# Spectra from sums and differences of mirrored steps, with new orders in the preparation and the routing

## Chip, cores and metric

The kernel runs on one core of a Trainium2 chip. The metric is the device time of one execution in microseconds (us). Before the change the median of 3 runs is 1136.09 us.

## The reference, cut to what matters

`x` is 2 x 512 x 512 and the context 2 x 8192 x 512, all in float32. Three layers are added to `x` one after the other. `LN` is a layer normalization over the last axis.

```
q, k, v = linear(linear(LN(x))), linear(linear(ctx)), ...
x = x + linear(softmax(q k^T / sqrt(512)) v + q)          # attention over 8192 steps
xn = LN(LN(x)) * ln_g + ln_b                              # state-space layer, 512 steps
u, z = split(xn @ in_w.T + in_b);  z = silu(z)
kernel[l, d] = sum_n exp(l * logA[d, n]) * C[d, n] * B[d, n] * dt[d]
y = irfft(rfft(u, 1024) * rfft(kernel, 1024))[:512]       # causal convolution over the steps
x = x + clip((y * z) @ out_w.T + out_b + LN(x), -10, 10)
e = argmax(softmax(LN(x) @ gate_w + gate_b))              # one of 8 experts for each token
x = x + LN(x) @ expert_w[e] + expert_b[e]
```

## The kernel before

Every large matrix product is made in three passes: an operand is split into a rounded part (`hi`) and a remainder (`lo`), both of type fp32r, and `PASSES` multiplies hi by hi, hi by lo and lo by hi. ScalarE writes the hi part from a PSUM bank, VectorE (DVE in the profile) subtracts it to make the lo part, and TensorE (PE) goes on with both. A product tile of 128 x 512 with a contraction of 512 is 12 matmuls. GpSimd (POOL) makes some lo parts from data in SBUF, and issues the gathers and scatters of the routing.

Each engine has an order written out by hand, with semaphores between them. `JOBS` lists the uses of the 8 PSUM banks in order, and `open_bank` makes TensorE wait until the use of the same bank 8 jobs earlier has been emptied (`evacuated` counts VectorE's, `copied` ScalarE's). The stages are:

- **Preparation** (`prepare`, 0 to about 148 us). Weights are folded into each other. TensorE transposes `qW`, makes `x_to_q`, transposes the normalized rows of batch 0 (`xT0`), makes the queries `q0`, transposes the rows of batch 1 (`xT1`), and makes `q_to_ctx`, `q1` and so on. `first_norm` on VectorE is 16 small instructions on 4 to 8 elements and four large ones. GpSimd meanwhile makes lo parts of `cW` (`lo_tiles`) and then the table of cosines and sines (`transform_table`, 31 us of small steps, result `dft`).
- **Attention of batch 0**, 64 steps of 24 matmuls each. Beside it ScalarE and VectorE sum the filter `kern` in 64 terms (`add_term`, counted by `term_added`).
- **Middle** (about 509 to 573 us). `turn_pooled` transposes the attention result and the input weights, `kernT` transposes the filter, `attend` adds the attention to `x`, `kernel_spectra` makes 8 spectra of the filter, the new rows are normalized and transposed (`normT`), then come `u`, `z` and `input_spectra(0)`, another 8 spectra.
- **Attention of batch 1**, with the complex products of batch 0 (`output_products`) on GpSimd.
- **Tail** (from about 929 us). The same for batch 1, with the products on VectorE (`outputs`, 20 instructions for each half of the frequencies), inverse transforms (`in_time`), the output projection (`project_out`), the last normalization, the choice of an expert for each token (`gate_logits`, `gate`, `route`), and 15 groups of 128 tokens: each is gathered, transposed (`turn_tokens`), multiplied with its expert's weights (`mix`) and scattered to the output.

The 512 steps are taken in two halves of 256 (`U0` and `U1`, for the filter `Ka` and `Kc`, from which `Ks` is made), each with a cosine and a sine part at 256 frequencies from the table `dft`. `spectrum` contracts over 256 steps, two tiles of 128:

```
for t in range(2):
    for a, c in PASSES:
        last = nc.tensor.matmul(dst[:], dft[:, a, t, m * P:(m + 1) * P], src[:, c, first + t, :], ...)
```

Of the kernel before, what the change touches and what calls it, by code (L numbers as in the profile page):

```python
# [12 lines left out]
P = 128  # L13
# [7 lines left out]
E = 8  # L21
# [47 lines left out]
def spectrum_jobs(b):  # L69
# [4 lines left out]
PREP_JOBS = (tiles("qWT", "x_to_q", "xT0") + ["vectors"] + tiles("kWT", "q0", "xT1", "q_to_ctx", "q1", "qc0", "vWT", "qc1")  # L74
# [10 lines left out]
             + ["logits@0"] + tiles_at(1, "ffnT")[2:] + ["logits@1", "logit_columns", "ranks", "slots"] + MIX_JOBS)  # L85
# [32 lines left out]
LOADS = [("hW", 1), ("oW", 0)]  # L118
# [10 lines left out]
def build(nc, x, ctx_in, hW, hb, cW, cb, qW, qb, kW, kb, vW, vb, oW, ob, A_log, B_param, C_param, log_dt,  # L129
          in_w, in_b, out_w, out_b, ln_g, ln_b, gate_w, gate_b, expert_w, expert_b, out):  # L130
    with ExitStack() as ctx:
# [39 lines left out]
        ident = sb("ident", [P, P])  # L171
        obB = sb("obB", [P, D])
# [60 lines left out]
        hit_group = h[1][:, 0:B * T * 2 * E].rearrange("p (i g) -> p i g", g=2 * E)  # L233
# [5 lines left out]
        sign = sb("sign", [P, 2])  # L239
        logA = sb("logA", [P, NS, T])  # L240
# [10 lines left out]
        in_q = [sem(f"in_q{half}") for half in range(2)]  # L251
        in_stage = [sem(f"in_stage{n}") for n in range(8)]
# [24 lines left out]
        u_biased = sem("u_biased")  # L277
        u_hi, u_lo = [sem(f"u_hi{b}") for b in range(B)], [sem(f"u_lo{b}") for b in range(B)]
# [70 lines left out]
        def evacuated_by(eng, name):  # L349

            if name in COPIED:
                eng.wait_ge(copied, COPIED[name])
            else:
                eng.wait_ge(evacuated, EVAC[name])

# [79 lines left out]
        def _(sp):  # L435
            def load(name, src):
                sp.dma_start(raw[BUF[name]][:], src).then_inc(in_stage[BUF[name]], 16)
# [4 lines left out]
            load("hW", matrix(hW))  # L442
# [163 lines left out]
            fixed_load(2)  # L606
            fixed_load(4)
            store_x(0)
            fixed_load(3)
# [17 lines left out]
        def _(pe):  # L627
# [47 lines left out]
            def turn_rows(job, src, k):  # L675
                dst = open_bank(job)
                for t in range(T):
                    last = nc.tensor.transpose(dst[:, t * P:(t + 1) * P], src[:, k, t * P:(t + 1) * P], ident[:])  # L678
# [7 lines left out]
            def prepare():  # L686
# [18 lines left out]
                products("q0.#", hlC, hlD)  # L705
                row_transposes("xT1.#", resid0, ROWS["x1"])
                split_of("cW")
                products("q_to_ctx.#", hlF, hlE)
# [123 lines left out]
            def spectrum(job, m, src, first):  # L832

                dst = open_bank(job)
                for t in range(2):
                    for a, c in PASSES:
                        last = nc.tensor.matmul(dst[:], dft[:, a, t, m * P:(m + 1) * P], src[:, c, first + t, :],  # L837
# [1443 lines left out]
```

## Time and profile before

| | before |
|---|---|
| median of 3 runs, us | 1136.09 (1134.95 to 1138.33) |
| the profiled execution, us | 1134.54, with a span of 1132.8 from its first to its last instruction |
| TensorE busy | 1093.9 us, 97% of the span |
| VectorE busy | 841.3 us, 74% |
| ScalarE, GpSimd busy | 530.5 and 537.5 us, 47% each |
| mean granted TensorE clock | 0.985 of full speed |

The profile lists, for each instruction or run of equal ones, its start, its length, its engine and line, the tile that it writes and those that it reads, and in brackets how long its engine stood idle before it and what ended that. A row with `x4` covers four instructions.

### The profile page before, as it was taken

To read this page: it belongs to the slowest core of one execution; us is meant where nothing else is said; L and a number is where in the kernel's file an instruction comes from. 1 tells how busy PE (TensorE), PEld (TensorE's weight loads), DVE (VectorE), ACT (ScalarE), POOL (GpSimd) and SP (SyncE) were. 2 spreads that over 40 slices of the span, in tenths; PEclk is the share of its full clock that TensorE was granted. 3 is DMA by queue.
4 is the path that set the end of the run, shared out by engine and by line. 5 is a ranking of instruction groups with operands and counts; after the bars stand their busy time and mean duration, and the time that the engine had idled before them with its cause. 6 is when DMAs were issued, how large, how long until landed. Compare 5 with 4: busy or idle time off the path is not lost.

```text
span 1132.8 us, 16497 instructions
## 1 busy us (share of the span) xinstructions
PE 1093.9 (97%) x4969; PEld 884.5 (78%) x4969; DVE 841.3 (74%) x1756; ACT 530.5 (47%) x1127; POOL 537.5 (47%) x588
## 2 busy tenths in 40 slices
PE   7999999999999999999999999999999999998498
PEld 5787877878888888888888888888888888886375
DVE  6963498799888888778357777776777657699584
ACT  4221056556555555533464444444444444356462
POOL 3700445345444544411266666665765632177253
PEclk8999999999999999999999999999999999999699
DMA  8211368977876787432429767766876541025991
GB/s 292 84 53 59 52 153 211 218 194 190 204 179 185 190 192 195 140 87 99 76 73 203 193 187 202 187 191 171 213 185 177 179 161 38 1 76 161 323 398 66
DMA packets 199351, 182.26 MB, mean 161 GB/s; under 512 B 17873, under 2 KB 144881, under 8 KB 199299
## 3 DMA queue, kind: packets, MB, share of 16 engines
q1 hardware_dynamic: 178658, 140.21, 48.3%
q10 hardware_dynamic: 17280, 31.46, 7.9%
q0 software_dynamic: 3360, 9.97, 2.4%
q8 instruction: 24, 0.39, 0.1%
q14 instruction: 29, 0.23, 0.1%
HBM read 141.73 MB, written 41.68 MB: 162 GB/s over the span
## 4 chain that ended last, share of the span: by engine, by line
PE 80%; DVE 8%; POOL 4%; DMA 3%; issue 3%; SPq 1%; ACT 1%; POOLq 0%; ACTq 0%; DVEq 0%
PE bank L644 39%; PE bank L783 28%; PE bank L1040 4%; PE bank L837 3%; PE bank L652 1%; PE bank L1026 1%; DMA stage<-in_L_xattn_hW_dram 1%; DVE h L1527 1%; DMA stage<-in_L_ffn_expert_w_dram 1%; DMA spectra<-in_ctx_dram 1%; PE bank L987 1%; PE bank L678 1%; POOL hl_C L2023 1%; PE bank L1045 1%; POOL hl_B L2039 1%
## 5 line engine op out<-in xcount | busy, mean ns | idle before, releaser
L1187 ACT ACTIVATE probs<-bank,nbias 128x512 f32<-128x512 f32 x128 | 88.1, 688 | 242.3 <-DVE nbias L1650 242.1
L783 PE MATMUL bank<-hl_F,probsT 128*128 128x512 f32 x768 | 190.4, 397 | 0.6 <-issue 0.4
L783 PE MATMUL bank<-hl_A,probsT 128*128 128x512 f32 x768 | 190.4, 396 | 0.0
L644 PE MATMUL bank<-hl_B,hl_D 128*128 128x512 f32 x768 | 185.7, 391 | 1.8 <-POOL hl_B L2039 1.4
L1645 DVE TENSOR_REDUCE mx<-bank 128x1 f32<-128x512 f32 x128 | 88.0, 687 | 133.9 <-PE bank L644 133.9
L644 PE MATMUL bank<-hl_C,hl_D 128*128 128x512 f32 x768 | 185.3, 390 | 0.0
L783 PEld LDWEIGHTS bank<-hl_F,probsT 128*128 128x128 f32 x768 | 144.1, 188 | 35.4 <-issue 0.8
L783 PEld LDWEIGHTS bank<-hl_A,probsT 128*128 128x128 f32 x768 | 144.1, 188 | 34.3 <-POOL hl_A L2032 0.2
L644 PEld LDWEIGHTS bank<-hl_B,hl_D 128*128 128x128 f32 x768 | 143.7, 188 | 34.1 <-issue 2.3
L644 PEld LDWEIGHTS bank<-hl_C,hl_D 128*128 128x128 f32 x768 | 144.1, 188 | 31.7 <-issue 0.3
L2032 POOL TENSOR_TENSOR hl_F<-stage,hl_F 128x512 fp32r<-128x512 f32 x64 | 84.7, 1323 | 162.2 <-ACT hl_F L1152 162.1
L2032 POOL TENSOR_TENSOR hl_A<-stage,hl_A 128x512 fp32r<-128x512 f32 x64 | 84.2, 1315 | 145.4 <-ACT hl_A L1152 145.4
L1691 DVE SCALAR_TENSOR_TENSOR rows<-rows,alpha,bank 128x512 f32<-128x512 f32 x128 | 90.9, 710 | 14.9 <-PE bank L783 14.9
L1662 DVE TENSOR_TENSOR probsT<-bank,probsT 128x512 fp32r<-128x512 f32 x128 | 87.3, 682 | 1.9 <-ACT probsT L1174 1.8
L1174 ACT ACTIVATE probsT<-bank 128x512 fp32r<-128x512 f32 x128 | 74.2, 580 | 10.8 <-PE bank L770 10.7
L1152 ACT ACTIVATE hl_F<-stage 128x512 fp32r<-128x512 f32 x64 | 40.4, 632 | 27.7 <-issue 18.2
L1152 ACT ACTIVATE hl_A<-stage 128x512 fp32r<-128x512 f32 x64 | 40.4, 632 | 27.6 <-issue 18.3
L2039 POOL TENSOR_TENSOR hl_C<-spectra,hl_C 128x512 fp32r<-128x512 f32 x32 | 40.9, 1292 | 22.9 <-ACT hl_C L1160 22.9
L2039 POOL TENSOR_TENSOR hl_C<-xb,hl_C 128x512 fp32r<-128x512 f32 x32 | 41.0, 1292 | 20.2 <-ACT hl_C L1160 20.2
L1667 DVE STREAM_TRANSPOSE bank<-resid 128x512 f32<-128x512 f32 x60 | 43.0, 716 | 9.4 <-DMA resid<-p_rows 9.4
L1683 DVE SCALAR_TENSOR_TENSOR lsum<-lsum,alpha,rsum 128x1 f32<-128x1 f32 x128 | 49.0, 383 | 0.0
L1699 DVE SCALAR_TENSOR_TENSOR zT<-h,cbdt,zT 128x512 f32<-128x512 f32 x64 | 46.6, 728 | 0.0
(419 smaller groups left out, 1862.6 us busy)
## 6 DMA issues: line engine op xcount, KB each, us to landing
p_rows<-probs ACTq DMA_DIRECT2D x120, 256.0 KB, 3.1
stage<-in_ctx_dram SPq DMA_DIRECT2D x112, 256.0 KB, 3.2
spectra<-in_ctx_dram SPq DMA_DIRECT2D x64, 256.0 KB, 5.9
xb<-in_ctx_dram SPq DMA_DIRECT2D x64, 256.0 KB, 5.9
resid<-p_rows SPq DMA_DIRECT2D x240, 64.0 KB, 2.1
h<-p_rows SPq DMA_DIRECT2D x120, 64.0 KB, 2.5
obB<-p_rows SPq DMA_DIRECT2D x120, 64.0 KB, 2.0
stage<-in_L_ffn_expert_w_dram SPq DMA_DIRECT2D x6, 1024.0 KB, 6.9
```

Of the source, the lines that this page charges most:

```text
L644: last = nc.tensor.matmul(dst, lhs[:, a, t, k * P:(k + 1) * P], rhs[:, c, t, :], start=(t == 0 and (a, c) == PASSES[0]), stop=(t == T - 1 ...
L783: last = nc.tensor.matmul(obank[u % 2][:], probsT[u % 2][:, a, j, :], nat[b][par][:, c, j, :], start=(j == 0 and (a, c) == PASSES[0]), sto ...
L1152: nc.scalar.activation(nat[b][par][:, 0, j, :], stage[par][:, j, :], ACT.Copy).then_inc(nat_hi, 1)
L1174: nc.scalar.activation(dst, src, ACT.Copy).then_inc(pT_hi, 1)
L1187: nc.scalar.activation(dst, src, ACT.Exp, bias=nbias[:, q:q + 1], scale=SCALE, accum_out=rsum[:, q:q + 1]).then_inc(probs_ready, 1)
L1645: nc.vector.tensor_reduce(mx[:, col], sbank[u % 2][:], AX_X, ALU.max).then_inc(stat_done, 1)
L1662: nc.vector.tensor_tensor(lo, src, hi, ALU.subtract).then_inc(pT_split, 1)
L1683: nc.vector.scalar_tensor_tensor(lsum[:, col], lsum[:, col], alpha[:, u:u + 1], rsum[:, col], ALU.mult, ALU.add).then_inc(sums_updated, 1)
L1691: nc.vector.scalar_tensor_tensor(rows[:, q, :], rows[:, q, :], alpha[:, u:u + 1], obank[u % 2][:], ALU.mult, ALU.add).then_inc(rows_added, 1)
L1699: nc.vector.scalar_tensor_tensor(kern[:, k, :], h[u % 2][:], weight, kern[:, k, :], ALU.mult, ALU.add).then_inc(term_added, 1)
L2032: nc.gpsimd.tensor_tensor(nat[b][par][:, 1, j, :], stage[par][:, j, :], nat[b][par][:, 0, j, :].bitcast(F32), ALU.subtract).then_inc(nat_s ...
L2039: nc.gpsimd.tensor_tensor(by_squares(ctxT[par][:, 1])[:, dd], square(squares[b][par], dd), by_squares(ctxT[par][:, 0])[:, dd].bitcast(F32) ...
```

## The change

1. **Spectra.** The two tiles of 128 steps of each half are first added and subtracted, with the nearer one in mirrored order. The sums give the cosine part and the differences the sine part, so `spectrum` contracts over 128 rows, 3 matmuls instead of 6, for all 24 spectra. The mirrored order comes for free in the transposes of the normalized rows (`flip` in place of `ident` for even tiles), in the lags of the filter (`lag_ramp`), in the reading of `z` (`gates`, two instructions instead of one) and in the inverse table (`inverse_table`, six instructions instead of four).
2. **Sums and differences** on VectorE: `fold_kernel` (4 instructions ahead of `lift(0)`), `inputs` (4 more) and `inputs_in_place` (4 more).
3. **The filter spectra** are turned in phase, by 8 instructions on ScalarE (`spectrum_parts`) and 8 on VectorE (`turn_spectra`), which wait for each other.
4. **The table** is half as large, and is made after both normalizations of the preparation (GpSimd waits for `rows_ready`); `lo_tiles("cW")` waits for the first one.
5. **Preparation:** `hW` is loaded in 4 transfers; `q_to_ctx` comes ahead of `xT1` on all engines.
6. **Tail:** the lo parts of `gated_hl[0]` move from GpSimd to VectorE; GpSimd's masks need two short instructions, and its lo parts of `W0` wait for the last product; SyncE loads `W3` ahead of `W4`; ScalarE rounds `W3` between two sums of rows; `gate_logits(1)` is one part, and the logits of batch 0 are turned ahead of it.
7. **Routing:** the first 8 groups are placed by `place_at(rank)` before the overflow groups are worked out; their gathers start at `indexed` 1. `split_expert_bias` moves behind `route`. `turn_tokens(1)` comes inside `mix(0)`.

```diff
-PREP_JOBS = (... + tiles("kWT", "q0", "xT1", "q_to_ctx", "q1", "qc0", "vWT", "qc1")
+PREP_JOBS = (... + tiles("kWT", "q0", "q_to_ctx", "xT1", "q1", "qc0", "vWT", "qc1")
...
             # sync
-            load("hW", matrix(hW))
+            load_tiles(stage[1], matrix(hW), in_h)        # for t in range(T): sp.dma_start(dst[:, t], src[:, t])
...
             fixed_load(1)
             fixed_load(2)
+            fixed_load(3)
             fixed_load(4)
             store_x(0)
-            fixed_load(3)
...
             # tensor
-            def spectrum(job, m, src, first):
+            def spectrum(job, m, src, n):
                 dst = open_bank(job)
-                for t in range(2):
-                    for a, c in PASSES:
-                        last = nc.tensor.matmul(dst[:], dft[:, a, t, m * P:(m + 1) * P], src[:, c, first + t, :], ...)
+                for a, c in PASSES:
+                    last = nc.tensor.matmul(dst[:], dft[:, a, 0, m * P:(m + 1) * P], src[:, c, n, :], ...)
...
             def middle():
                 turn_pooled(0)
-                pe.wait_ge(term_added, TERMS)
-                transposes("kernT.#", kern)
+                turn_kernel()                             # waits for kern_folded 4
...
-                gate_logits(1, 2)
-                turn_logits()
+                turn_logits(0)
+                gate_logits(1, 1)
+                turn_logits(1)
                 rank_tokens()
-                place_tokens()
+                place_tokens("slots.0", 1, 0, E)
+                place_tokens("slots.1", 2, E, E)
                 turn_tokens(0)
                 for g in range(GROUPS):
-                    if g + 1 < GROUPS:
+                    if 0 < g < GROUPS - 1:
                         turn_tokens(g + 1)
                     mix(g)                                # mix(0) calls turn_tokens(1) after its first tile
...
             # scalar
+            def spectrum_parts():
+                for c in range(2):
+                    for n, m in enumerate((Ka, Ks)):
+                        ...
+                        if c + n > 0:
+                            act.wait_ge(spectrum_turned, 2 * (2 * c + n))
+                        nc.scalar.activation(probs[0][:], m[:, 2 + c, :], ACT.Copy, scale=turn[:, 2 + c:3 + c]).then_inc(part_put, 1)
+                        nc.scalar.activation(probs[1][:], m[:, c, :], ACT.Copy, scale=turn[:, 2 + c:3 + c]).then_inc(part_put, 1)
...
                 weights(1)
                 weights(2)
-                for t in range(2, T):
-                    sum_rows(t)
+                sum_rows(2)
+                weights(3)
+                sum_rows(3)
                 means()
-                weights(3)
...
             # vector
             def inputs():
-                for k in range(T):
-                    filled_by(dve, f"u.{k}@0")
-                    nc.vector.tensor_tensor(uT[:, k, :], bank_of(f"u.{k}@0")[:], ubB[:], ALU.add).then_inc(evacuated, 1)
+                for n in range(2):
+                    near, far = 2 * n, 2 * n + 1
+                    for k in (near, far):
+                        filled_by(dve, f"u.{k}@0")
+                        nc.vector.tensor_tensor(uT[:, k, :], bank_of(f"u.{k}@0")[:], ubB[:], ALU.add).then_inc(evacuated, 1)
+                    dve.wait_ge(evacuated, EVAC[f"u.{far}@0"])
+                    nc.vector.tensor_tensor(h[n][:], uT[:, far, :], uT[:, near, :], ALU.add).then_inc(u_folded, 1)
+                    nc.vector.tensor_tensor(uT[:, far, :], uT[:, far, :], uT[:, near, :], ALU.subtract).then_inc(u_folded, 1)
+
+            def fold_kernel():
+                dve.wait_ge(term_added, TERMS)
+                for n in range(2):
+                    ...
+                    nc.vector.tensor_tensor(h[n].rearrange("p (t m) -> p t m", t=T), far, near, ALU.add).then_inc(kern_folded, 1)
+                    nc.vector.tensor_tensor(far, far, near, ALU.subtract).then_inc(kern_folded, 1)
+
+            def turn_spectra():
+                for n in range(2 * 2):
+                    c, m = n // 2, (Ka, Ks)[n % 2]
+                    cosine = turn[:, c:c + 1]
+                    dve.wait_ge(part_put, 2 * n + 2)
+                    nc.vector.scalar_tensor_tensor(m[:, c, :], m[:, c, :], cosine, probs[0][:], ...).then_inc(spectrum_turned, 1)
+                    nc.vector.scalar_tensor_tensor(m[:, 2 + c, :], m[:, 2 + c, :], cosine, probs[1][:], ...).then_inc(spectrum_turned, 1)
...
             def middle():
+                fold_kernel()
                 lift(0)
...
                 lo_rows("normT.#@0", hlF)
+                turn_spectra()
                 inputs()
...
             # vector, tail
                 gate_output(0, range(2, T))
-                outputs(1, range(1, 5))
+                outputs(1, range(1, 3))
+                for k in range(T):
+                    gated_lo(0, k)
+                outputs(1, range(3, 5))
...
                 scale_outputs()
-                split_expert_bias()
                 gate()
                 route()
+                split_expert_bias()
...
             # vector, route
-                nc.vector.tensor_reduce(rank, hit_value, AX_X, ALU.add)
+                link(nc.vector.tensor_reduce(rank, hit_value, AX_X, ALU.add))
+                place_at(rank)
...
+                filled_by(dve, "slots.0")
+                nc.vector.tensor_scalar(gather_rows[:, 0:E], bank_of("slots.0")[:, 0:E], ...).then_inc(indexed, 1)
...
             # gpsimd
+            pool.wait_ge(rows_ready, ROWS["x0"] + 1)
             lo_tiles("cW", zT, hlE)
+            pool.wait_ge(rows_ready, ROWS["x1"] + 1)
             transform_table()
...
                 add_out_bias(0)
-                gated_lo()
                 routing_masks()
+                pool.wait_ge(product_step, PRODUCTS * (TRIPS + 2))
+                lo_tiles("W0", raw[BUF["W0"]], weights_hl[0])
                 add_out_bias(1)
```

## Rows read from the trace of the kernel before

**Rows 1.** The page: TensorE's busy time, share of the span and instructions.

```profile
PE 1093.9 (97%) x4969; PEld 884.5 (78%) x4969; DVE 841.3 (74%) x1756; ACT 530.5 (47%) x1127; POOL 537.5 (47%) x588
```

**Rows 2.** Timeline, TensorE in the preparation (start, length, what, idle before).

```profile
29.90 11.20 PE L644 MATMUL bank<-hl_D,hl_C 128*128 128x512 f32 x48 [0.31 <-DVE hl_D L1464]
...
43.53 2.91 PE L678 MATMUL bank<-ident,resid 128*128 128x128 f32 x16 [2.44 <-DVE hl_F L1421]
...
46.09 12.27 PE L644 MATMUL bank<-hl_E,hl_F 128*128 128x512 f32 x48
...
58.19 11.04 PE L644 MATMUL bank<-hl_D,hl_C 128*128 128x512 f32 x48
```

**Rows 3.** Timeline of all engines, 10 to 17 us.

```profile
10.46 2.19 ACT L1112 ACTIVATE hl_B<-stage 128x512 fp32r<-128x512 f32 x4 [1.64 <-DMA stage<-in_L_xattn_hW_dram]
...
11.86 13.90 PE L644 MATMUL bank<-hl_A,hl_B 128*128 128x512 f32 x48 [4.08 <-DVE hl_B L1509]
...
16.65 1.22 DVE L1489 TENSOR_SCALAR seed<-var 128x4 int32<-128x4 int32 x1
```

**Rows 4.** Timeline of VectorE, about 40 us.

```profile
39.55 3.23 DVE L1498 TENSOR_SCALAR resid<-xb,mv,rstd 128x512 f32<-128x512 f32 x4
...
42.70 2.47 DVE L1421 TENSOR_TENSOR hl_F<-bank,hl_F 128x512 fp32r<-128x512 f32 x4
```

**Rows 5.** Windows in the preparation (busy by engine, PEclk, DMA share, GB/s).

```profile
10.00:15.00 5.00, 3.14 (x7) 2.48 (x8) 3.88 (x7) 2.19 (x4) 0.00 (x0) 0.59 1.04 390
...
45.00:50.00 5.00, 5.00 (x20) 4.12 (x19) 4.96 (x8) 2.48 (x5) 4.76 (x6) 0.66 0.48 173
```

**Rows 6.** Timeline of the middle stage, 509 to 563 us.

```profile
509.76 0.75 DVE L1691 SCALAR_TENSOR_TENSOR rows<-rows,alpha,bank 128x512 f32<-128x512 f32 x1 [3.81 <-PE bank L783]
...
516.55 11.13 PE L644 MATMUL bank<-hl_E,hl_A 128*128 128x512 f32 x48
...
527.52 11.05 PE L837 MATMUL bank<-hl_F,dft 128*128 128x512 f32 x48
...
532.35 1.91 DVE L1498 TENSOR_SCALAR rows<-xb,mv,rstd 128x512 f32<-128x512 f32 x4
...
538.60 0.75 DVE L1790 SCALAR_TENSOR_TENSOR qc<-resid,sign,bank 128x512 f32<-128x512 f32 x1 [0.55 <-PE bank L837]
...
540.41 11.18 PE L644 MATMUL bank<-hl_B,hl_F 128*128 128x512 f32 x48
...
552.36 0.63 ACT L1262 ACTIVATE hl_A<-spectra 128x512 fp32r<-128x512 f32 x1 [2.09 <-DVE spectra L1764]
...
553.07 1.29 POOL L2145 TENSOR_TENSOR hl_A<-spectra,hl_A 128x512 fp32r<-128x512 f32 x1 [1.43 <-ACT hl_A L1262]
...
562.31 11.04 PE L837 MATMUL bank<-hl_A,dft 128*128 128x512 f32 x48
```

**Rows 7.** Timeline of the tail, up to the first wait for outputs.

```profile
978.17 1.29 DVE L376 TENSOR_TENSOR probs<-qc,spectra 128x512 f32<-128x512 f32 x2 [2.59 <-issue]
...
1001.54 1.67 DVE L376 TENSOR_TENSOR spectra<-probs,obB 128x512 f32<-128x512 f32 x1
...
1012.07 0.98 PE L875 MATMUL bank<-probsT,hl_B 128*128 128x256 f32 x6 [0.22 <-DVE hl_B L1810]
```

**Rows 8.** Timeline of the tail, from the expert weights to the first mix.

```profile
1035.95 2.19 ACT L1341 ACTIVATE hl_F<-stage 128x512 fp32r<-128x512 f32 x4 [3.54 <-DMA stage<-in_L_ffn_expert_w_dram]
...
1040.23 3.59 PE L987 MATMUL bank<-spectra,gate_raw 128*8 128x512 f32 x8 [2.82 <-ACT spectra L1224]
...
1053.71 0.22 DVE L1906 TENSOR_TENSOR ssm_in<-onehot,bank 128x64 f32<-128x64 f32 x1 [1.58 <-PE bank L1010]
...
1057.19 1.22 DVE L1928 TENSOR_TENSOR dft<-ssm_in,ssm_w 128x1024 fp32r<-128x1024 f32 x1
...
1060.37 0.17 DVE L1932 TENSOR_SCALAR gather_rows<-bank 128x15 int32<-128x15 f32 x1 [1.06 <-PE bank L1017]
...
1069.69 4.28 PE L1040 MATMUL bank<-hl_C,probsT 128*128 128x512 f32 x12
```

More of the change, by code:

```diff
@@ L71, in spectrum_jobs @@
     return at(b, *[f"{n}.{c}" for c in range(2) for n in ("U0r", "U0i", "U1r", "U1i")])
-PREP_JOBS = (tiles("qWT", "x_to_q", "xT0") + ["vectors"] + tiles("kWT", "q0", "xT1", "q_to_ctx", "q1", "qc0", "vWT", "qc1")
+PREP_JOBS = (tiles("qWT", "x_to_q", "xT0") + ["vectors"] + tiles("kWT", "q0", "q_to_ctx", "xT1", "q1", "qc0", "vWT", "qc1")
              + tiles("ctx_to_v", "oWT") + ["key_row.0", "key_row.1", "x_bias", "key_bias"] + tiles("ctx_to_x", "qo0")
@@ L84 @@
              + tiles_at(0, "x_ssm")[2:] + tiles_at(1, "x_ssm") + tiles_at(0, "ffnT") + tiles_at(1, "ffnT")[:2]
-             + ["logits@0"] + tiles_at(1, "ffnT")[2:] + ["logits@1", "logit_columns", "ranks", "slots"] + MIX_JOBS)
+             + ["logits@0"] + tiles_at(1, "ffnT")[2:] + ["logits@1", "logit_columns", "ranks", "slots.0", "slots.1"] + MIX_JOBS)
 JOBS = PREP_JOBS + MID_JOBS + TAIL_JOBS
@@ L251, in build @@
         in_q = [sem(f"in_q{half}") for half in range(2)]
+        in_h = [sem(f"in_h{t}") for t in range(T)]
         in_stage = [sem(f"in_stage{n}") for n in range(8)]
@@ L435, in _, with load_tiles @@
         def _(sp):
+            def load_tiles(dst, src, landed):
+                for t in range(T):
+                    sp.dma_start(dst[:, t], src[:, t]).then_inc(landed[t], 16)
             def load(name, src):
@@ L705, in prepare @@
                 products("q0.#", hlC, hlD)
+                split_of("cW")
+                evacuated_from("kWT.3")
+                products("q_to_ctx.#", hlF, hlE)
                 row_transposes("xT1.#", resid0, ROWS["x1"])
-                split_of("cW")
-                products("q_to_ctx.#", hlF, hlE)
                 evacuated_from("xT1.3")
@@ L1010, in rank_tokens, with place_tokens @@
                 nc.tensor.matmul(dst[:, B * T * E:2 * B * T * E], ones, flat, start=True, stop=True).then_inc(filled, 1)
-            def place_tokens():
-                pe.wait_ge(ranked, 1)
-                dst = open_bank("slots")
+            def place_tokens(job, count, first, width):
+                pe.wait_ge(ranked, count)
+                dst = open_bank(job)
                 for n in range(B * T):
-                    last = nc.tensor.matmul(dst[:, 0:2 * E], place[:, n, :], numbered[:, n, :], start=(n == 0), stop=(n == B * T - 1))
+                    last = nc.tensor.matmul(dst[:, 0:width], place[:, n, :], numbered[:, n, first:first + width],
+                                            start=(n == 0), stop=(n == B * T - 1))
                 last.then_inc(filled, 1)
@@ L1041, in mix @@
                                          start=(t == 0 and (a, c) == PASSES[0]), stop=False)
+                    if g == 0 and t == 0:
+                        turn_tokens(1)
                 if g == 0:
```

231 lines of the change are left out of this document (138 added, 93 removed).

## The prediction

> **What bounds the kernel now.** I read the page first. TensorE is busy for 97% of the span [rows 1]. The two attention passes are long runs of matmuls that the change does not touch, so the whole gain or loss lies in the preparation, the middle and the tail. For these I read the timeline engine by engine, looking for the wait that TensorE ends on, because a matmul that is removed is worth something only where TensorE does not then wait for VectorE.
>
> Preparation: the first products start 4.08 us late, on the lo part of `hW` [rows 3]. The clock was granted at 0.59 in that stretch [rows 5], so 48 matmuls take 13.90 us where the same 48 take 11.20 later [rows 2]. A second idle time of 2.44 us stands ahead of `xT1`; then the clock is 0.66 [rows 5] and 48 matmuls take 12.27 us [rows 2]. Middle: TensorE is nearly gapless, but the `u` products at 540.41 end a VectorE path (attention added, statistics, rows, four filter spectra, lo part), since `normT` ends on VectorE [rows 6]. Tail: VectorE runs the products one after the other from 978.17 [rows 7], and TensorE meets it at 1012.07. Then logits wait 2.82 us for ScalarE, which had stood idle 3.54 us for `W3` [rows 8].
>
> **The change part by part.** One matmul is 11.04 / 48 = 0.230 us [rows 6]. 24 spectra lose 3 each: 72 x 0.230 = 16.6 us of TensorE. How much is kept must be worked out by stage.
>
> *Preparation.* (a) `hW` by tiles. ScalarE waited 1.64 us for the one transfer and started at 10.46; VectorE's first lo part came 0.66 later and the product at 11.86 [rows 3]. With tiles landing in turn, the start is set by VectorE, which is done with `qWT` about 1.3 us before that product. So 1.3 us, and a busy TensorE should be back at full clock sooner: of the 13.90 - 11.20 = 2.7 us that the slow clock costs, I take 1.3 back. From both sides: 0 (all tiles land as late as the one) and 1.3 + 2.7 = 4.0. I take 2.6 at the start of `q0`.
> (b) GpSimd waits for both normalizations. In the first, a `TENSOR_SCALAR` on 4 elements took 1.22 us and the next three about as much, while GpSimd worked; a `TENSOR_SCALAR` of that size takes 0.17 when it doesn't (the one at 1060.37) [rows 8]. That hides under TensorE. In the second, the four large ones took 3.23 us [rows 4] against 1.91 for the same four at 532.35 [rows 6]. VectorE starts it about 2.6 us earlier by (a), and gains 1.3 + 1.0 on the way, so the lo parts of `kWT`, at 42.70 [rows 4], start near 37.8 and end 2.47 later, at 40.3.
> (c) `q_to_ctx` goes first. It needs those lo parts, so it starts at 40.3 in place of 46.09 [rows 2]. `q0` ends near 29.90 - 2.6 + 11.1 = 38.4, so 1.9 us of idling remain, less than the 2.44 that was followed by a slow clock; I take full clock. It ends at 51.4; `xT1` takes 1.9 us; then `q1` needs its last lo part (0.6 on ScalarE, 0.7 on VectorE): start at 54.6 against 58.19. **Gain 3.6 us**. If the clock falls, 12.27 - 11.04 = 1.2 to 1.7 us less. Everything behind, the loads of squares too, hangs on this chain and shifts with it. The table ends near 37.7 + 26 = 64, and is first needed at about 82; with no cover it would cost nothing until it took 44 us.
>
> *Middle.* (d) `fold_kernel`, four instructions with an effective 0.62 (2.47 / 4) [rows 4] = 2.5 us, stands ahead of `lift(0)` on VectorE, after the row at 509.76. The transposes of the weights use banks that VectorE empties, so `attend` at 516.55 slides to about 519. (e) Filter spectra: 24 x 0.230 = 5.5 us less on TensorE. But `u` hangs on VectorE: from 527.52, where `attend` ends, to the first `u` product at 540.41 are 12.9 us. Without waiting for spectra, VectorE needs 532.35 + 1.91 - 527.52 = 6.7 for statistics and rows, 4 x 0.69 for the filter spectra (0.75 each alone, row at 538.60) and 0.7 for the lo part: 10.2. 12.9 - 10.2 = 2.7, minus the 2.5 of (d): **gain 0.2**. Bounds: -2.5 (the fold fully exposed) and 3.0. (f) Input spectra: 5.5 us less, if the sums and differences are there. After the lo parts of `normT` (about 542), phase turning is four rounds of two ScalarE (0.63 + 0.55) and two VectorE instructions (0.74 + 0.66), 2.7 us each, the first round's ScalarE part covered: VectorE is free at 551.5. `inputs` is 8 x 0.62 + 0.1 = 5.1: 556.6. Then ScalarE 0.63 (at 552.36) and GpSimd 1.29 (at 553.07) [rows 6] for the last tile, with the tile before it queued: 559.8. The spectra start at 562.3 and want the second half 1.4 later; cover is 3.9 us, and the `z` products are what hides it. ScalarE then has `gates` (1.3 + 4 x 0.95) behind the rounding: until 564.6, and 8 copies of 0.52: 568.8, while TensorE needs the fourth at 567.8 to go on. **Gain 5.4 us**. Bounds 0 to 5.5.
>
> The Trainium skill (SBUF — State Buffer, Who interferes with whom) says that a VectorE instruction with two SBUF inputs and a GpSimd instruction that reads SBUF exclude each other for the whole instruction. By that, the sums and differences could each wait for one of GpSimd's lo parts; the sum with two such waits would put the last tile at 562.4, still within the cover.
>
> *Tail.* (g) The third set of spectra saves 5.5 us that VectorE does not use: it starts its products only when the first two spectra are copied. `inputs_in_place` ends 1.3 later than now, its ScalarE partner starts earlier; the products start at 977.8, 0.4 us early. 28 instructions later nothing has changed; then four lo parts are added (4 x 0.6 = 2.4), and the waits go that GpSimd caused: 1.67 us for a 0.69 us instruction at 1001.54 [rows 7], 3.1 us in all. The second outputs are ready near 1010.6, where TensorE meets them at 1012.07 [rows 7]: **1.4 us**. Bounds -2 and 5. (h) `W3` is issued some 15 us earlier, so the 2.82 us of waiting at 1040.23 go [rows 8], minus 0.9 because `gate_logits(1)` now waits for all its tiles: **1.9 us**, bounds 0 and 2.8. With (g) and 0.1 the ranks come 3.4 us early. (i) Routing. Before, from the first instruction on the ranks at 1053.71 to `gather_rows` at 1060.37 are 6.7 us [rows 8]. After: 0.6, then `place_at` 1.22 (the 1057.19 row), TensorE's 8 matmuls 1.9 with three short links beside them, so 3.8 us: 2.9 early. But VectorE must then work out the overflow (3.5), wait for `slots.1` (2) and split the bias (2.6), free at ranks + 12.4, when the first gathered tile wants its lo part at ranks + 11.4. `mix(0)` starts at ranks + 13.1 against 1069.69 - 1053.71 = 16.0 now: 2.9, less 0.9 for `turn_tokens(1)` inside it: **2.0 us**, bounds 0 and 3. Its 14 followers run at TensorE's pace and keep it.
>
> Sum: 3.6 + 0.2 + 5.4 + 1.4 + 1.9 + 0.1 + 2.0 = 14.6 us. The profiled execution took 1134.54, 1.55 below the median of 1136.09: 1134.54 - 14.6 = 1119.9, and for the median 1121.5. I predict **1121.5 us**.
>
> **Rivals.**
> - *Phase turning is not hidden.* If a round takes 3.9 us in place of 2.7, the cover of 3.9 is gone, and from there each microsecond of a round costs four. With rounds of 5.3 the whole 5.4 is lost: 1127. Against: all durations have rows. Chance 12%.
> - *`hW` gains nothing.* Three more issues on SyncE (0.46 us each) push `x[0]` and `cW` back, and the DMA share is 1.04 in that stretch [rows 5], so tiles may land no sooner. Then (a) is 0 and `q0` starts at 29.9; (b) and (c) keep a part: 1124.0. Chance 15%. The Trainium skill (SBUF — State Buffer, Summary: rules for kernel authors) asks for one transfer on 128 partitions and not several; by that rule this case would be the likeliest.
> - *Routing gives back.* VectorE's later bias split, or the stores of the rows that the gathers wait for, end last: (i) and (h) are 0, 1125.5. Chance 8%.
> - *Slower.* In the attention passes VectorE has about 0.5 us free in a step of 5.54. If the second pass is entered in another phase to GpSimd, and one short instruction per step is caught behind a GpSimd one (1.22 in place of 0.17 is 1.05) [rows 3, 8], the step grows by 0.55: 64 x 0.55 = 35 us, 1156. It decides from 15 us / 64 = 0.23 us a step. Nothing in the first pass, entered from another side, shows it. Chance 3%.
> - *The change doesn't do what it says*: TensorE falls back to a pace of one copy per spectrum. A copy is 0.60 against 3 x 0.230 = 0.69; it would need to be longer. Chance 2%, counted with the first.
>
> **How the numbers follow.** Forecast 58% (1118.5 to 1124.0), the rivals 14, 15, 8 and 3%, and 2% for better than all. The range reaches to the phase-turning rival and to the upper bounds of (a), (e), (g): **1115.5 to 1127.5**. What a measurement of this kernel can tell from no change is about 0.3%, 3.4 us. Only parts of the middle rivals together end within it: faster 94%, same 3%, slower 3%.
>
> **What would show it.** `q1` starts near 54.6. `attend` starts 2 to 3 us later relative to the end of attention, `u` at the same distance, the second attention pass 5.5 us sooner. Input spectra have no idle time ahead of them. In the tail, the product rows are all 0.69. `gather` starts 6 us after the onehot, not 9. I am wrong if TensorE waits for `u_lo` ahead of the input spectra, if the PEclk falls in a stretch where it was 1.00, or if steps of attention are longer than 5.54.

## The result, and the profile after

The changed kernel took 1126.13 us (median of 5; 1124.40 to 1128.57), the kernel before 1136.08 in the same comparison: ratio 0.9917, 95% interval 0.9901 to 0.9933. In a second comparison (after_again, below) it was 0.9914 (0.9894 to 0.9933). The medians are 9.9 us apart in both comparisons, and the ratios make it 9.4 and 9.8 us, where 14.6 were forecast: in the range of 1115.5 to 1127.5, but 2.1 us above the 1118.5 to 1124.0 to which the forecast gave 58%. The profiled execution is the one of 1126.13; its span is 1124.3 against 1132.8 (an execution 1.5 us below its median), so 8.5 us are to be found in the trace.

The page, TensorE's line, against [rows 1]:

```profile
PE 1081.0 (96%) x4897; PEld 873.5 (78%) x4897; DVE 846.6 (75%) x1784; ACT 535.8 (48%) x1145; POOL 523.0 (47%) x583
```

TensorE lost 12.9 us of busy time and the kernel 8.5. Timeline of TensorE in the preparation:

```profile
10.33 12.52 PE L657 MATMUL bank<-hl_A,hl_B 128*128 128x512 f32 x48 [2.52 <-DVE hl_B L1562]
...
26.65 11.17 PE L657 MATMUL bank<-hl_D,hl_C 128*128 128x512 f32 x48
39.96 12.75 PE L657 MATMUL bank<-hl_E,hl_F 128*128 128x512 f32 x48 [2.15 <-DVE hl_F L1474]
52.55 1.91 PE L692 MATMUL bank<-ident,resid 128*128 128x128 f32 x16
56.52 12.80 PE L657 MATMUL bank<-hl_D,hl_C 128*128 128x512 f32 x48 [2.06 <-DVE hl_D L1517]
69.16 3.11 PE L657 MATMUL bank<-hl_A,hl_B 128*128 128x512 f32 x13
```

`q0` starts 3.25 us sooner than in [rows 2], `q_to_ctx` (39.96) 6.1 sooner, `q1` (56.52) only 1.7 sooner, and `qc0` starts at 69.16 against 69.07 before. Two idle times of 2.1 us now stand where one of 2.44 stood, and both products behind them are slow. Windows of TensorE (busy, count, granted clock, DMA share, GB/s):

```profile
42.00:44.00 2.00, 2.00 (x6) 0.51 0.74 264
44.00:46.00 2.00, 2.00 (x11) 1.00 0.92 318
58.00:60.00 2.00, 2.00 (x6) 0.50 0.00 0
```

Six matmuls in 2 us at 0.5 (1.2 GHz), eleven at 1.00 (2.4 GHz). Timeline of VectorE ahead of `q1`:

```profile
53.39 0.69 DVE L1486 TENSOR_TENSOR hl_B<-bank,hl_B 128x512 fp32r<-128x512 f32 x1 [2.04 <-ACT hl_B L1095]
53.99 2.48 DVE L1517 TENSOR_TENSOR hl_D<-bank,hl_D 128x512 fp32r<-128x512 f32 x4
```

The four lo parts of `xT1` can't begin before the last one of `q_to_ctx`, and TensorE waits for all four. Timeline of the middle:

```profile
509.83 0.75 DVE L1744 SCALAR_TENSOR_TENSOR rows<-rows,alpha,bank 128x512 f32<-128x512 f32 x1 [3.81 <-PE bank L799]
...
514.00 3.19 PE L665 MATMUL bank<-ident,stage 128*128 128x128 f32 x16 [2.47 <-DVE hl_B L1525]
...
519.36 11.14 PE L657 MATMUL bank<-hl_E,hl_A 128*128 128x512 f32 x48
530.34 5.60 PE L852 MATMUL bank<-hl_F,dft 128*128 128x512 f32 x24
...
540.37 11.17 PE L657 MATMUL bank<-hl_B,hl_F 128*128 128x512 f32 x48 [1.20 <-DVE hl_F L1517]
...
544.89 0.75 DVE L1839 SCALAR_TENSOR_TENSOR qc<-qc,turn,probs 128x512 f32<-128x512 f32 x1 [1.47 <-ACT probs L1273]
...
556.50 1.77 DVE L1822 TENSOR_TENSOR spectra<-spectra 128x512 f32<-128x512 f32 x1
...
559.38 1.30 POOL L2251 TENSOR_TENSOR hl_A<-spectra,hl_A 128x512 fp32r<-128x512 f32 x1
562.26 5.60 PE L852 MATMUL bank<-hl_A,dft 128*128 128x512 f32 x24
567.70 2.66 PE L657 MATMUL bank<-hl_B,hl_D 128*128 128x512 f32 x11
```

Against [rows 6]: `attend` 2.8 later, `u` where it was, input spectra without an idle time ahead of them and half as long. The second attention starts 5.49 us sooner (567.70; 573.19 before) and takes 358.66 us to the transposes of its last rows, where it took 358.74. Timeline of the tail:

```profile
971.99 1.29 DVE L385 TENSOR_TENSOR probs<-qc,spectra 128x512 f32<-128x512 f32 x2 [1.41 <-ACT spectra L1250]
...
1004.95 0.98 PE L899 MATMUL bank<-probsT,hl_B 128*128 128x256 f32 x6 [1.48 <-DVE hl_B L1895]
...
1030.74 3.59 PE L1010 MATMUL bank<-spectra,gate_raw 128*8 128x512 f32 x8
...
1039.88 0.59 ACT L1277 ACTIVATE h<-bank 8x512 f32<-8x512 f32 x1 [3.77 <-PE bank L1010]
...
1044.52 0.22 DVE L1992 TENSOR_TENSOR ssm_in<-onehot,bank 128x64 f32<-128x64 f32 x1 [0.80 <-PE bank L1033]
...
1048.42 0.17 DVE L2002 TENSOR_SCALAR gather_rows<-bank 128x8 int32<-128x8 f32 x1 [1.45 <-PE bank L1040]
...
1050.83 1.24 POOL L2297 DMA_INDIRECT spectra<-mixed,gather_rows  x1 [19.21 <-DMA mixed<-zT]
...
1057.28 1.09 PE L1050 MATMUL bank<-ident,spectra 128*128 128x128 f32 x4 [3.14 <-DMA spectra<-mixed,gather_rows]
...
1059.87 1.62 PE L1064 MATMUL bank<-hl_C,probsT 128*128 128x512 f32 x3 [1.50 <-DVE probsT L2052]
...
1065.42 0.49 PE L1071 MATMUL bank<-dft,selected 16*128 16x512 f32 x1
```

Against [rows 7, 8]: the second outputs come 7.1 us sooner, the ranks 9.2, the gather's indices 11.9, but `mix(0)` 9.8, and its last matmul (1065.42) 8.5, since it was at 1073.89. The gather was released by a store (`mixed<-zT`), not by its indices.

| us ahead of before, at | measured | forecast |
|---|---|---|
| `qc0` (end of the preparation's chain) | -0.1 | 3.6 |
| `u` | 0.0 | 3.8 |
| second attention | 5.5 | 9.2 |
| second outputs | 7.1 | 10.6 |
| ranks | 9.2 | 12.6 |
| end of `mix(0)` | 8.5 | 14.6 |

### The profile page after: what moved, and what is told of

Same layout as the page of the kernel before. It is cut to its first block, busy times and chain, and to the rows that moved or that the text cites. A ratio compares the mean times of both kernels' runs of the same rounds, so it can differ in the third digit from the quotient of the medians.

```text
span 1124.3 us, 16407 instructions
## 1 busy us (share of the span) xinstructions
PE 1081.0 (96%) x4897; PEld 873.5 (78%) x4897; DVE 846.6 (75%) x1784; ACT 535.8 (48%) x1145; POOL 523.0 (47%) x583
## 4 chain that ended last, share of the span: by engine, by line
PE 79%; DVE 11%; issue 4%; POOL 2%; DMA 2%; ACT 1%; SPq 1%; POOLq 0%; ACTq 0%; DVEq 0%
PE bank L657 41%; PE bank L799 28%; PE bank L1064 4%; PE bank L665 1%; DVE probs L385 1%; PE bank L1050 1%; DVE h L1580 1%; PE bank L1010 1%; DMA spectra<-in_ctx_dram 1%; PE bank L1071 1%; POOL hl_B L2137 1%; DMA resid<-p_rows 1%; PE bank L743 0%; POOL hl_F L2130 0%; PE bank L852 0%
## 5 line engine op out<-in xcount | busy, mean ns | idle before, releaser
L1168 ACT ACTIVATE h<-resid,logA 128x512 f32<-128x512 f32 x64 | 45.4, 709 | 0.0
```

## The experiments

### Preparation

**ctx_last**: the order alone undone, on TensorE, ScalarE and VectorE.

```diff
-tiles("kWT", "q0", "q_to_ctx", "xT1", "q1", ...
+tiles("kWT", "q0", "xT1", "q_to_ctx", "q1", ...
...
                 products("q0.#", hlC, hlD)
+                row_transposes("xT1.#", resid0, ROWS["x1"])
                 split_of("cW")
-                evacuated_from("kWT.3")
                 products("q_to_ctx.#", hlF, hlE)
-                row_transposes("xT1.#", resid0, ROWS["x1"])
...                                                   # ScalarE and VectorE in the same order
```

> Undoes one edit of the preparation, the order: xT1 is turned ahead of q_to_ctx again, hW by tiles and GpSimd's two waits stay. Theory (the new order costs the gain): q0 ends at 37.8 us as now; the transposes of xT1 need only the banks that VectorE frees with the lo parts of kWT from 38.1 on, so TensorE idles about 0.3 us and not 2.15, xT1 ends near 40.4, q_to_ctx takes 11.04 at full clock and q1 starts near 51.5 in place of 56.52: 5.0 us faster than the changed kernel, 1121. Rival 1 (the order is worth something, and the gain was lost to other work): q1 starts at 56.5 or later, time unchanged or up to 2 us longer. Rival 2 (the clock falls near 40 us whatever the order, with the burst of loads that begins there): q_to_ctx takes 12.3 to 12.8 although TensorE hardly idled, q1 at 53, 3.4 us faster.

1119.98 us, ratio 0.9882 (0.9866 to 0.9899). Timeline of TensorE:

```profile
38.30 2.42 PE L692 MATMUL bank<-ident,resid 128*128 128x128 f32 x16 [0.35 <-DVE hl_F L1473]
40.76 11.12 PE L657 MATMUL bank<-hl_E,hl_F 128*128 128x512 f32 x48
51.72 11.04 PE L657 MATMUL bank<-hl_D,hl_C 128*128 128x512 f32 x48
62.60 11.04 PE L657 MATMUL bank<-hl_A,hl_B 128*128 128x512 f32 x48
```

`q1` at 51.72 as expected, `qc0` at 62.60: 6.56 us sooner than in the changed kernel, 4.80 by `q1`'s start and 1.76 by its clock. Another 1.6 of it is the clock of `q_to_ctx` (12.75 for 11.12), so the order by itself costs 3.2 us. By the ratios (0.9917 and 0.9882, two chips) it is 4.0 us, with 2.6 to either side; the trace of the changed kernel is one in which both products were slow, which is not always so, as filled_gaps tells. With the old order, the copies of `xT1` hide under `q_to_ctx`.

**ctx_last_one_hW**: as ctx_last, `hW` in one transfer, for which ScalarE waits once.

```diff
-            load_tiles(stage[1], matrix(hW), in_h)
+            sp.dma_start(stage[1][:], matrix(hW)).then_inc(in_h[0], 16)
```

> As ctx_last, and hW is one transfer again. Theory (tiles of hW are worth what the start of the first product shows): x_to_q at 11.9 in place of 10.33 and 13.9 us long in place of 12.52, q0 at 29.9 in place of 26.65, everything to q1 3.2 us later than in ctx_last: 3.2 us slower than ctx_last. Rival (the tiles' gain is the work of GpSimd's waits, which free VectorE ahead of q0): q0 at 27.5 or earlier, under 1 us slower than ctx_last.

1120.99 us, ratio 0.9894 (0.9878 to 0.9910). Timeline of TensorE, `x_to_q` and `q0`:

```profile
10.95 12.78 PE L653 MATMUL bank<-hl_A,hl_B 128*128 128x512 f32 x48 [3.12 <-DVE hl_B L1557]
...
27.54 11.17 PE L653 MATMUL bank<-hl_D,hl_C 128*128 128x512 f32 x48
```

`q0` is 0.80 us behind ctx_last (26.74), not 3.2: tiles are worth 0.8 in these two traces (the medians are 1.0 us apart, within the intervals). The one transfer let ScalarE start at 9.54 here and at 10.46 in [rows 3]; and `x_to_q` took 13.90 before, 12.52 to 12.80 in ten traces of the changed kernel and its variants and 13.58 to 14.09 in three, according to how long TensorE kept to 4 matmuls in a microsecond before it went on with 6. Of the 3.25 us of the first comparison 0.8 are the tiles', and up to 1.2 belong to GpSimd's waits (`q0` at 28.22 without them and at 27.04 with them, in the next experiment). The rest, 1.3 us or more, belongs to no edit that was tested.

**ctx_last_pool_free**, and later **all_four_pool_free** beside **all_four** (below): GpSimd's two waits out.

```diff
-            pool.wait_ge(rows_ready, ROWS["x0"] + 1)
             lo_tiles("cW", zT, hlE)
-            pool.wait_ge(rows_ready, ROWS["x1"] + 1)
             transform_table()
```

> As ctx_last, but GpSimd no longer waits for the two normalizations (lo parts of cW and the table start when their inputs are there). Theory (GpSimd's work beside the norms costs VectorE 2 to 3 us in the second norm, which TensorE ends on): q0 still starts within 0.5 us of ctx_last's, the lo parts of kWT are 1.5 to 2.5 us later, q_to_ctx and q1 too: 1.5 to 2.5 us slower than ctx_last. Rival (the contention hides under q0): same time as ctx_last within 0.5 us.

> As all_four, and GpSimd again does not wait for the two normalizations. Theory (in ctx_last_pool_free x_to_q was 1.5 us longer only because the clock came back later in that execution; the small instructions of 1.2 us hide under TensorE): same time as all_four within 1 us, rows of the first norm near 21.6 in place of 17.3 and no TensorE wait behind them. Rival (the waits are worth the 2.6 us by which ctx_last_pool_free was slower than ctx_last): 2 to 2.6 us slower, again with a longer x_to_q.

1122.57 us, 0.9900 (0.9885 to 0.9915), against 0.9882; and 1116.95 us, 0.9844 (0.9830 to 0.9858), against 0.9821. In the first of them the longer `x_to_q` (14.09) hid the matter; the second settles it. Timeline of all_four_pool_free:

```profile
17.27 1.22 DVE L1545 SCALAR_TENSOR_TENSOR newton<-newton,var 128x4 f32<-128x4 f32 x1
...
28.22 11.17 PE L657 MATMUL bank<-hl_D,hl_C 128*128 128x512 f32 x48 [1.14 <-DVE hl_D L1516]
40.34 2.42 PE L692 MATMUL bank<-ident,resid 128*128 128x128 f32 x16 [0.94 <-DVE hl_F L1473]
42.79 11.17 PE L657 MATMUL bank<-hl_E,hl_F 128*128 128x512 f32 x48
```

`x_to_q` took 12.77 (12.80 in all_four), and `q0` now waits 1.14 us for VectorE, whose instructions of 1.22 no longer hide. `q_to_ctx` is 1.7 us later than all_four's 41.08. My expectation of no difference was wrong: once TensorE is sooner, the waits are worth 1.7 us there and 2.9 in the medians. The difference between the two traces grows to 2.2 us by `attend` and to 3.0 by the tail; why it grows during the attention passes stays open.

**filled_gaps**: the changed order, with discarded matmuls for its two idle times: nine ahead of the last tile of `q0`, which moves into the first, and nine ahead of `q1`.

```diff
+            def filler(dst, lhs, rhs, n):
+                for m in range(n):
+                    nc.tensor.matmul(dst[:], lhs[:, 0, m % T, 0:P], rhs[:, 0, m % T, :], start=(m == 0), stop=(m == n - 1))
...
+                    if k == T - 1:
+                        filler(open_bank("q0.3"), hlC, hlD, 9)
...
+                filler(open_bank("q1.0"), hlF, hlE, 9)
                 evacuated_from("xT1.3")
```

> The changed kernel, order and all, with work put into TensorE's two idle gaps of the preparation whose result is thrown away: 9 extra matmuls ahead of q0's last product (2.07 us) and 9 ahead of q1 (2.07 us), each into a bank that the next product starts anew. Nothing starts sooner by it. Theory (the slow stretches follow the idle gaps): q_to_ctx starts at 39.9 as before but takes 11.04 in place of 12.75, the gap ahead of q1 is filled too, and q1 takes 11.05 in place of 12.80: 3.4 us faster. Rival (the clock falls with the burst of loads at 40 us, or when the chip draws more, and not for idling): q_to_ctx and q1 keep 12.7 to 12.8, and the time is that of the changed kernel or longer by the part of the extra matmuls that does not fit, 0 to 0.5 us.

1122.78 us, ratio 0.9907 (0.9893 to 0.9921). Timeline of TensorE (L704 is the filler):

```profile
35.19 2.20 PE L704 MATMUL bank<-hl_D,hl_C 128*128 128x512 f32 x9
...
40.22 11.14 PE L657 MATMUL bank<-hl_E,hl_F 128*128 128x512 f32 x48
51.19 1.91 PE L692 MATMUL bank<-ident,resid 128*128 128x128 f32 x16
52.86 2.30 PE L704 MATMUL bank<-hl_E,hl_F 128*128 128x512 f32 x9
55.16 11.18 PE L657 MATMUL bank<-hl_D,hl_C 128*128 128x512 f32 x48
66.17 11.04 PE L657 MATMUL bank<-hl_A,hl_B 128*128 128x512 f32 x48
```

Nothing starts sooner by the fillers, yet both products run at full clock and `qc0` comes 3.0 us sooner, while the loads of 40 to 50 us are there as before. A window of filled_gaps, to be laid beside the one of the changed kernel above:

```profile
42.00:44.00 2.00, 2.00 (x11) 1.00 0.65 244
```

The rival of the loads falls: here they run beside a granted clock of 1.00, and in the changed kernel the clock was 0.50 from 58 to 60 us with no load at all. The medians show less than the 3.4 us expected (the ratio fell by 0.001, 1.1 us, within the intervals), and the other traces tell why: the clock does not fall each time. After an idle time of 2.12 to 2.15 us, `q_to_ctx` took 12.73 to 12.77 in three of seven traces of the changed order and 11.16 or 11.17 in four; after 2.06 us, `q1` took 12.76 to 12.80 in six and 11.17 in one. With 0.94 us or less ahead, all twelve such products took 11.04 to 11.18. One trace of fillers could be chance by itself; 9 of 14 against none of 12 is what shows that the idle time costs the clock.

### Middle

**fold_early**, beside **after_again**, the changed kernel itself, on one chip with the two of the routing.

```diff
-                for u in (UN - 2, UN - 1):
-                    weighed_rows(TRIPS - 1, u)
+                weighed_rows(TRIPS - 1, UN - 2)
+                if kernel_terms:
+                    fold_kernel()
+                weighed_rows(TRIPS - 1, UN - 1)
...
             def middle():
-                fold_kernel()
```

> The changed kernel itself, beside the next three on one chip, as their base. Expected as before: 0.992 of the kernel before, q_to_ctx and q1 at 12.7 us each behind an idle time of 2 us, the first gather 2.2 us behind its indices.

> The changed kernel with the four instructions of fold_kernel moved from behind the last attention row to between the last two, where VectorE idled 3.81 us. Theory (the fold's 2.5 us stand in full on the path to u, and the 5.5 us that the filter spectra gave up are what hides them): the last row stays at 509.8, the transposes that waited at 514.00 start near 511.5, attend near 516.9 in place of 519.36, u and all behind it 2.5 us sooner: 2.5 us faster. Rival (u hangs on something else of VectorE's or on spectra): attend is sooner, but u moves by less than 1 us.

after_again 1125.03 us, 0.9914 (0.9894 to 0.9933); fold_early 1123.49, 0.9905 (0.9885 to 0.9926). Timeline of fold_early:

```profile
509.35 1.91 PE L692 MATMUL bank<-ident,rows 128*128 128x128 f32 x16
511.32 2.54 PE L665 MATMUL bank<-ident,stage 128*128 128x128 f32 x16
...
516.34 11.16 PE L657 MATMUL bank<-hl_E,hl_A 128*128 128x512 f32 x48
```

The wait of 2.47 us is gone. From the transposes of the last rows to `u` are 28.03 us against 30.43 in after_again: 2.40, as expected, though the medians alone (1.5 us apart) would not prove it.

**kernel_twice** and **input_and_third_twice**: each of the named spectra worked out twice, the first one overwritten.

```diff
             def spectrum(job, m, src, n):
                 dst = open_bank(job)
+                if job[0] == "K":      # or kind(job)[0] == "U"
+                    for a, c in PASSES:
+                        nc.tensor.matmul(dst[:], dft[:, a, 0, m * P:(m + 1) * P], src[:, c, n, :],
+                                         start=((a, c) == PASSES[0]), stop=((a, c) == PASSES[-1]))
```

> The changed kernel with each of the eight filter spectra worked out twice, the first time into the bank that the second starts anew: 24 matmuls and 5.5 us more on TensorE, the length of before. Theory (with the fold ahead of it, u hangs on TensorE's spectra as much as on VectorE, so the halving pays for the fold): filter spectra end near 541.4 in place of 535.9, normT and u start 4.5 us later, all behind it too: 4.5 us slower than the changed kernel. Rival (u hangs on VectorE alone, as the prediction's small gain of 0.2 could be read): u moves by under 1 us.

> The changed kernel with the eight input spectra of the middle and the eight of the tail worked out twice in the same way, 5.5 us more TensorE in each place. Theory: in the middle all of it shows (TensorE goes from the spectra straight into the second attention, which starts 5.5 us later); in the tail 1.4 us shows, since VectorE's products start when the second spectrum is copied, two doubled spectra later, and TensorE then waits for them anyway (2.44 and 1.48 us of idling): 6.9 us slower in all. Rival: 11 us (TensorE is the bound in the tail too) or 5.5 (the copies set the start of the products).

kernel_twice 1127.34 us, 0.9932 (0.9916 to 0.9948); input_and_third_twice 1132.30, 0.9984 (0.9971 to 0.9997). The rows that count, of kernel_twice:

```profile
509.88 1.91 PE L692 MATMUL bank<-ident,rows 128*128 128x128 f32 x16
...
543.66 1.66 PE L657 MATMUL bank<-hl_B,hl_F 128*128 128x512 f32 x6
```

33.78 us to `u` where after_again has 30.43: 3.35 later. But 0.47 of that lies ahead of `attend`, which starts 9.87 us after those transposes here and 9.40 there, because the transposes behind the idle time ran slower. From `attend` to `u` are 23.91 us here, 21.03 in after_again and 21.01 in the changed kernel: 2.9 of the 5.5 show (4.5 expected). In input_and_third_twice the second attention starts 63.19 us after those transposes against 57.77, 5.4 in full; in the tail, from `u` (959.13) to the second outputs (1010.57) are 51.44 us against 50.00 in the changed kernel (954.95 to 1004.95): 1.4 of 5.5. By the ratios the two kernels are 2.0 and 7.9 us behind after_again, which the intervals can't tell from the 2.9 and 6.8 of the traces.

### Routing

**norm_first** and **norm_first_bias_back**:

```diff
-                copy_logits(1)
-                for b in range(B):
-                    normalize_outputs(b)
+                normalize_outputs(0)
+                copy_logits(1)
+                normalize_outputs(1)
...
+                split_expert_bias()      # second kernel only
                 gate()
                 route()
-                split_expert_bias()
```

> The changed kernel with ScalarE normalizing the first half of the output rows ahead of its copy of logits(1), in 3.77 us in which it idled, not behind. Theory (the gathers wait for the stores of the normalized rows, not for their indices): the stores are issued 2.8 us sooner, the first gather goes 0.1 us behind its indices in place of 2.2, the first transposes of tokens come 2.15 us sooner, and mix(0) 1.9 us sooner, then held by VectorE's bias split: 1.9 us faster. Rival (the gathers wait for the queue behind the stores or for loads in flight): gather and mix(0) move by less than 0.5 us, no gain.

> As norm_first, and the split of the experts' bias is back ahead of the gate, where VectorE idles 5.8 us. Theory: mix(0) another 0.2 to 0.3 us sooner than in norm_first, 2.2 us faster than the changed kernel in all. Rival (the late bias split, ending at ranks + 12.6 us, is what gives the routing's gain back): norm_first gains nothing and this one gains 1.5 us or more over it.

1123.93 us, 0.9905 (0.9889 to 0.9921), and 1122.65 us, 0.9892 (0.9877 to 0.9908). Timeline of norm_first:

```profile
1046.01 0.22 DVE L1992 TENSOR_TENSOR ssm_in<-onehot,bank 128x64 f32<-128x64 f32 x1 [1.64 <-PE bank L1033]
...
1051.01 1.24 POOL L2297 DMA_INDIRECT spectra<-mixed,gather_rows  x1 [18.74 <-DVE gather_rows L2002]
...
1059.17 1.62 PE L1064 MATMUL bank<-hl_C,probsT 128*128 128x512 f32 x3 [2.39 <-DVE probsT L2052]
```

The gather is released by its indices, 1.10 us behind their instruction's start as before the change ([rows 8] and a gather at 1061.47), not the 0.1 that I expected, and 2.41 in the changed kernel. It starts 5.00 us after the ranks (6.31 in the changed kernel, 5.23 in after_again), and `mix(0)` at ranks + 13.16 (15.35 and 14.51). So the wait for the stores is worth 0.2 to 1.3 us. The rest is the gather itself, from its start to TensorE's transposes: 6.45 us in the changed kernel, 4.69 here, 4.73 before. It begins 4.2 us behind the issue of the loads of `W6` and `W7` in the changed kernel, 6.6 here and 6.3 before; in six traces with 4.0 to 4.2 us the gather took 6.45 to 6.72, and in five with 5.6 to 6.6 it took 4.69 to 5.71. That they compete is argued from this, not shown. The wait of 2.39 above is for VectorE, which ended the bias split at 1058.4. With the split moved too, the wait is 1.50, but that gather took 5.71 us and `mix(0)` starts at ranks + 13.31; in all_four it took 4.93, and `mix(0)` starts at ranks + 12.53. The step from 0.9905 to 0.9892 is within the intervals: what the late split costs, up to 0.6 us by all_four's trace, stays unproven.

### All together

**all_four** is ctx_last, fold_early, norm_first and the bias split ahead of the gate in one kernel.

> All edits that gained, on the changed kernel: xT1 turned ahead of q_to_ctx, the fold ahead of the last row, rows normalized ahead of logits(1), the bias split ahead of the gate. Theory (they stand in three stages one behind the other and add up): by stages q1 4 to 5 us sooner, u another 2.4, mix(0) another 2.1: 9 us faster than the changed kernel, 0.984 of the kernel before. Rival (the second attention, entered sooner in another phase, or the tail gives a part back): 0.988.

1114.04 us, ratio 0.9821 (0.9806 to 0.9836): 20 us faster than before and, by the ratios (0.9914 - 0.9821), 10.6 faster than the changed kernel. By stages of the two traces, changed kernel against this: `qc0` 69.16 and 62.96, `u` 540.37 and 531.38, second attention 567.70 and 558.72, second outputs 1004.95 and 995.90, `mix(0)` 1059.87 and 1047.94. The gains of the preparation and the middle are kept through the attention passes, and the routing adds its own.

## Why the prediction was right, and where not

Direction and range held, 1126.13 in 1115.5 to 1127.5, because the middle and the tail up to the ranks came out term by term. That the time stayed in the range, 1.4 us from its end, is in part the width of the range: it reached up to the rival of the phase turning, which did not happen. Two terms of the sum failed, and they make the whole of the difference. One of the prediction's own signs of being wrong came too: the granted clock fell where it had been 1.00 (0.50 from 58 to 60 us, where 48 matmuls took 11.04 before).

- **(a)** `q0` 2.6 us sooner was forecast and 3.25 came, but the tiles are worth 0.8 and GpSimd's waits, which the sum gave nothing here, up to 1.2; the rest is when the transfer landed and how long the first product ran slowly. The rival in which `hW` gains nothing was nearer to the truth about the edit. The Trainium skill (SBUF — State Buffer, Summary: rules for kernel authors) asks for one transfer, not several; here four were 0.8 us ahead of one in the traces, in a stretch with the DMA at a share of 1.0; the likely reason is that the first consumer starts on one tile.
- **(b)** The lo parts of `kWT` were forecast at 37.8 and stood at 37.39. "That hides under TensorE" was right of the trace before but for 0.31 us ([rows 2]), and wrong of a TensorE that starts `x_to_q` 1.6 us sooner and does it in 12.77 us for 13.90 (1.14 us of waiting in all_four_pool_free).
- **(c) failed**, by 3.7 us, in two sentences. "I take full clock": `q_to_ctx` started at 39.96 (forecast 40.3) but ended 1.2 us late at 12.75. And "`q1` needs its last lo part": it needs all four, queued behind the last lo part of `q_to_ctx` on VectorE, 2.06 us and not 1.3. That second idle time then took `q1`'s clock too, 1.76 us, which the sum did not have at all. The price of a fallen clock was named (1.2 to 1.7 us) and put at nothing. The order was counted as a gain because `q_to_ctx` starts sooner; ctx_last shows that it costs 6.6 us of trace, 3.2 of them without the clock. The other order has no idle time above 0.35 us, and there was all the gain: the waits that were the reason for the new order were already gone by (a) and (b).
- **(d), (e)** `attend` 2.8 later, `u` 0.04 sooner; forecast 0.2. fold_early and kernel_twice give the two halves: the fold costs 2.4, or 2.8 where the transposes behind its idle time run slower (5.36 us to `attend` and not 5.02), as in the changed kernel, and the halved filter spectra give back 2.9 of their 5.5 (23.86 us from `attend` to `u` before, 21.01 after). That makes 0.1, and so it came: from the transposes of the last rows to `u` are 30.75 us, and 30.85 before. The forecast had the sum right and missed that the fold's 2.4 could be had too: VectorE idles 3.81 us ahead of the last row, and that row was in [rows 6].
- **(f)** 5.5 against 5.4. The rounds of turning took 2.87 us each (2.7), the last lo part ended at 560.68 (559.8), the spectra started at 562.26 (562.3). Of the cover of 3.9 us, 2.9 were left. The Trainium skill (SBUF — State Buffer, Who interferes with whom) has such sums exclude GpSimd's lo parts for a whole instruction: one difference took 1.77 us in place of 0.69 and two lo parts 1.74 in place of 1.30, so the trace agrees, and it stayed under the cover. The price of the rival on the phase turning was a little off: by its own rule (four times the excess of a round over 2.7) 3.9 us of cover are gone at rounds of 3.7, not 3.9, and the 5.4 with them at 5.0, not 5.3.
- **(g), (h)** 7.12 - 5.56 (the shift at the start of the tail, the `attend` of batch 1 at 934.18 for 939.74) = 1.56 us against 1.4, then 2.07 more at the ranks against 2.0 (1.9 + 0.1); but 0.6 of it is the clock, since seven of the ranks' matmuls took 0.92 us for 1.54 before (1.63 in after_again). (h) itself brought 1.4 to 1.5. All product rows are 0.68 to 0.78. No run undoes `W3`'s place or that of the lo parts, so these shares are read from the two traces only.
- **(i) failed**: 2.0 forecast, -0.7 came between ranks and the end of `mix(0)` (9.19 to 8.47): its start gained 0.6 for 2.9 (ranks + 15.35; 15.98 before), and from there to its last matmul are 5.55 us for 4.20, 1.35 and not 0.9 for `turn_tokens(1)`. The indices were ready 3.90 us after the ranks as forecast, and the gather waited for the stores of the normalized rows, whose ScalarE work stands behind the copy of the logits. The rival named the stores and got 8% with no look at ScalarE's queue; what it took from the sum is (i), and (h) stayed. With the wait gone, `mix(0)` starts at ranks + 13.16, where 13.1 was forecast.

Sum of the misses: 3.7 + 2.7 = 6.4; with 0.3 from the rest in the other direction, 14.6 becomes the 8.5 of the trace.

## What to carry to other kernels

When a product is moved ahead to fill an idle time, ask what hid behind it: here the copies that the next product needs ran under it, and moved out of its cover they cost an idle time and the clock. Price an order after the other edits are in, not against the old trace. For every transfer that reads what a store wrote, follow the store back through its engine's queue before counting on earlier indices.

## What the runs showed of the hardware

- TensorE's clock fell to 1.2 GHz after idle times of only 2.06 to 2.15 us in 9 of 14 cases in the preparation, at a price of 1.6 to 1.8 us each, and never there after 0.94 us or less (12 cases). The same kernel showed both (`q_to_ctx` 12.75 and 11.17), so a forecast of such a gap is a chance of 1.7 us, not a figure.
- It is so elsewhere too. Ahead of `u` stands an idle time of 1.20 us in twelve traces, and in one of them (ctx_last_pool_free) the clock fell behind it. In the tail an idle time of 2.44 to 2.46 us was followed by 24 matmuls in 5.68 to 5.71 us in eight traces and in 7.30 to 7.33 in four (after_again is one); there it cost nothing, since TensorE waited for the second outputs anyway (7.18 us from that start with either clock). The two rows, of ctx_last_pool_free and of after_again:

```profile
538.65 12.77 PE L657 MATMUL bank<-hl_B,hl_F 128*128 128x512 f32 x48 [1.20 <-DVE hl_F L1516]
997.91 7.31 PE L657 MATMUL bank<-hl_E,hl_F 128*128 128x512 f32 x24 [2.46 <-issue]
```

- At the start, the time until TensorE reached its full pace varied from run to run: 48 matmuls took 12.52 to 14.09 us in 13 traces, with a start between 10.27 and 10.45 in all but one. The granted clock does not always tell: in five of these traces it is recorded as 1.00 throughout, while TensorE does 4 matmuls in a microsecond at first and 6 later. One trace of before can't carry a term of that size.
- Four-element VectorE instructions took 1.18 to 1.26 us beside GpSimd's large subtractions and 0.17 without; why they hold each other up was not tested by itself.
